# Output bias of the cross attention added on GpSimd, and a new order of the pipelined step, in a one-core decoder layer

## What is computed

```
x = layernorm(x + self_attention(x))            # 16 heads of 8, scores times a decay, softmax
x = layernorm(x + cross(x, ctx))                # below
x = layernorm(x + mixture_of_experts(x))        # layernorm, router, top 2 of 8 experts
cross(q, v):  vp = v @ Wv.T + bv
              A  = softmax(q_h^T k_h / sqrt(128))        # per head, 8 x 8
              out = (vp_h A) @ Wo.T + bo
```

## Time and profile before

| | |
|---|---|
| median of 3 runs | 750.74 us (748.93 to 753.12) |
| the profiled execution | 747.79 us, of which the span in the trace is 746.1 us |
| first block | up to 400 us of the span |
| busy in the span: PE, DVE, ACT, POOL | 573.0, 523.6, 395.0, 393.3 us |
| granted TensorE clock, mean | 0.913 of full speed |

### The profile page before, as it was taken

One profiled execution on the slowest core, in us unless ns is written; L12 is line 12 of the kernel. 1 busy time (PEld: TensorE's weight loads), 2 busy tenths in 40 slices (PEclk: granted clock), 3 DMA queues, 4 the chain that ended last, 5 costly groups with the idle time before them and its releaser, 6 DMA issues. The chain is left out here.

```text
span 746.1 us, 18061 instructions
## 1 busy us (share of the span) xinstructions
PE 573.0 (77%) x5145; PEld 453.1 (61%) x5145; DVE 523.6 (70%) x1567; ACT 395.0 (53%) x1076; POOL 393.3 (53%) x751
## 2 busy tenths in 40 slices
PE   1599999999999999999630698888888888880000
PEld 1256777777777777777520587777777787770000
DVE  1268888888888888888323377677777677760877
ACT  1177888888888888888310344444444444440000
POOL 4073568777777777778670034334344444342444
PEclk9999999999999999999755799999999999995555
DMA  4252121212121211110000555555555555531442
GB/s 149 67 67 66 37 69 48 77 44 73 53 76 48 68 55 45 51 48 17 16 29 7 145 161 170 156 162 163 156 166 165 169 168 160 162 98 34 118 117 84
DMA packets 75650, 70.20 MB, mean 94 GB/s; under 512 B 7809, under 2 KB 58561, under 8 KB 75553
## 3 DMA queue, kind: packets, MB, share of 16 engines
q1 hardware_dynamic: 65264, 55.40, 25.4%
q0 software_dynamic: 5392, 11.01, 5.0%
q10 hardware_dynamic: 4896, 2.64, 1.2%
HBM read 53.85 MB, written 15.17 MB: 93 GB/s over the span
## 5 line engine op out<-in xcount | busy, mean ns | idle before, releaser
L1092 ACT ACTIVATE x2c<-ps_m,prt 128x256 f32<-128x256 f32 x117 | 55.5, 475 | 139.8 <-PE ps_m L1057 139.8
L737 DVE TENSOR_TENSOR sc<-ps_s,decay 128x512 f32<-128x512 f32 x128 | 84.7, 685 | 28.7 <-PE ps_s L522 28.4
L1068 PEld LDWEIGHTS ps_t<-wot,hid 128*128 128x128 f32 x624 | 93.3, 192 | 12.7 <-DVE hid L1128 4.0
L1043 POOL DMA_INDIRECT expert_out<-yt,dest x78 | 82.5, 1057 | 34.0 <-issue 27.8
L1055 PE MATMUL ps_m<-xg,w2t 128*128 128x256 f32 x234 | 73.9, 398 | 32.2 <-DVE hid L1124 29.3
L1068 PE MATMUL ps_t<-wot,hid 128*128 128x128 f32 x624 | 95.8, 277 | 2.7 <-DVE hid L1128 1.9
L522 PE MATMUL ps_s<-kbd,qT 32*128 32x512 f32 x256 | 75.9, 670 | 9.3 <-DMA kbd<-key_image 6.7
L586 ACT ACTIVATE pT<-ps_t 128x512 f32<-128x512 f32 x128 | 72.7, 593 | 16.7 <-PE ps_t L533 16.7
L748 DVE TENSOR_REDUCE rowmax<-sc 128x8 f32<-128x1024 f32 x64 | 78.1, 1220 | 0.4
L659 ACT ACTIVATE sc<-sc,rowmax 128x128 f32<-128x128 f32 x256 | 77.9, 390 | 0.0
L533 PE MATMUL ps_t<-ident,sc 128*128 128x128 f32 x512 | 77.1, 284 | 0.0
(11 more groups left out here) (202 smaller groups left out, 1307.2 us busy)
## 6 DMA issues: line engine op xcount, KB each, us to landing
w2t<-in_L_ffn_W_dram SPq DMA_DIRECT2D x39, 256.0 KB, 2.7
w1t<-in_L_ffn_W_dram SPq DMA_DIRECT2D x39, 256.0 KB, 2.9
wot<-in_L_ffn_Wo_dram SPq DMA_DIRECT2D x39, 256.0 KB, 3.6
kbd<-key_image SPq DMA_DIRECT2D x32, 256.0 KB
xst<-expert_in SPq DMA_DIRECT2D x39, 130.0 KB, 2.1
g<-expert_out SPq DMA_DIRECT2D x32, 128.0 KB, 2.2
call<-in_ctx_dram SPq DMA_DIRECT2D x8, 256.0 KB, 6.5
key_image<-kT SPq DMA_DIRECT2D x32, 64.0 KB, 2.0
```

The costliest lines, as they stand in the source:

```text
L737: dve.tensor_tensor(sc[:, 2 * (b % 2) + i // 2, j:j + 4, :], ps_s[:, i % 2, :, :], decay[:, :].unsqueeze(1).to_broadcast([P, 4, S]), ALU.m ...
L1043: pool.indirect_dma_start(ys_dram[:, :], bass.IndirectOffsetOnAxis(ap=dest[:, n, a:a + 1], axis=0), yt[:, par, a, :], None).then_inc(y_out ...
L1068: mm = pe.matmul(ps_y[par][:, a * P:(a + 1) * P], hid[:, par, c, a * P:(a + 1) * P], wot[:, par, c, :], start=(c == 0 and a == 0), stop=(c ...
```

## The change

The bias is added by POOL: `biased_rows(b)` writes `x1b = x1 + bo_row` into a buffer of its own, with two slots, and `second_sum` has two products in place of three: `oT` with Wo, and `ident` with `x1b`. The matrix `first` and its two memsets go. ACT's `norm1` waits for `x1b_ready` in place of `x_out` before it writes `x1` again.

The lists of all four engines have a new order. On PE the four `mix` and `mix_sums` now stand together behind `score(s + 1, 0)`, and `second_out`, `values`, `ranks`, `second_sum` and `trans_p(s, 0)` follow them; `keys` and `queries` stand later in the step, `trans_p(s - 1, 3)` ahead of `trans_p(s - 1, 2)`. On ACT `norm4` moves from the front to behind `copy_o`, and `copy_p(b, 1)` comes before `copy_p(b, 0)`. On POOL `shift` stands near the end of the list and `router_rows` behind it. The lists of ACT and DVE count their steps from another start; one step more is in the range for that.

```diff
@@ -80,7 +80,6 @@
         router_w = sb("router_w", [P, E])
         ident = sb("ident", [P, P])
         ones = sb("ones", [P, P])
-        first = sb("first", [P, P])
         earlier = sb("earlier", [P, P])
         decay = sb("decay", [P, P])
         wq = sb("wq", [P, D])
@@ -114,6 +113,7 @@
         attT = sb("attT", [P, D])
         st1 = sb("st1", [P, 6]); mv1 = sb("mv1", [P, 2]); rs1 = sb("rs1", [P, 1])
         x1 = sb("x1", [P, 2, D])
+        x1b = sb("x1b", [P, 2, D])
         cT = sb("cT", [P, S])
         vpT = sb("vpT", [P, S])
         gm = sb("gm", [P, D])
@@ -170,7 +170,7 @@
         gram = sem("gram"); gm_ready = sem("gm_ready"); gmax_ready = sem("gmax_ready"); gexp = sem("gexp")
         ginv = sem("ginv"); gA_ready = sem("gA_ready")
         o_done = sem("o_done"); oT_ready = sem("oT_ready"); x_out = sem("x_out")
-        stat2 = sem("stat2"); mean2 = sem("mean2"); eps2 = sem("eps2"); nm_ready = sem("nm_ready"); nm1_ready = sem("nm1_ready"); gained = sem("gained"); scaled = sem("scaled"); rstd2 = sem("rstd2"); x2_ready = sem("x2_ready")
+        stat2 = sem("stat2"); mean2 = sem("mean2"); eps2 = sem("eps2"); nm_ready = sem("nm_ready"); x1b_ready = sem("x1b_ready"); nm1_ready = sem("nm1_ready"); gained = sem("gained"); scaled = sem("scaled"); rstd2 = sem("rstd2"); x2_ready = sem("x2_ready")
         xc_ready = sem("xc_ready"); xf_ready = sem("xf_ready")
         stat4 = sem("stat4"); mean4 = sem("mean4"); eps4 = sem("eps4"); rstd4 = sem("rstd4"); xhat_ready = sem("xhat_ready")
         f_trans = sem("f_trans"); fT_ready = sem("fT_ready"); routed = sem("routed")
@@ -191,7 +191,7 @@
             before(eng, s, min(b, B - 1) + 1)
 
 
-        first_step, last_step = -2, B + 6
+        first_step, last_step = -2, B + 7
 
         with nc.Block() as block:
 
@@ -259,10 +259,7 @@
 
                 pool.memset(shift2[:, 0:1], EPS).then_inc(cst, 1)
                 pool.memset(shift2[:, 1:2], EPS * EPS / (1.0 + EPS)).then_inc(cst, 1)
-                pool.memset(first[:, :], 0.0).then_inc(cst, 1)
-                pool.wait_ge(cst, 11)
-                pool.memset(first[0:1, :], 1.0).then_inc(cst, 1)
-                pool.wait_ge(cst, 12)
+                pool.wait_ge(cst, 10)
 
                 pool.memset(ones[:, :], 1.0).then_inc(rcst, 1)
                 pool.memset(fill[:, :, :], 0.0).then_inc(rcst, 1)
@@ -332,6 +329,11 @@
                     pool.wait_ge(scaled, b + 1)
                     pool.tensor_tensor(xf[:, b % 2, :], xc[:, b % 2, :], offset_row[:, :], ALU.add).then_inc(xf_ready, 1)
 
+                def biased_rows(b):
+                    pool.wait_ge(x1_ready, b + 1)
+                    before(pool, x_out, b - 1)
+                    pool.tensor_tensor(x1b[:, b % 2, :], x1[:, b % 2, :], bo_row[:, :], ALU.add).then_inc(x1b_ready, 1)
+
                 def choices(b):
                     pool.wait_ge(oh_ready, b + 1)
                     before(pool, ranked, b)
@@ -362,16 +364,17 @@
                                                 xhat[:, b, :], None).then_inc(scattered, 16)
 
                 for s in range(first_step, last_step + 1):
-                    if ever(s - 7): place(s - 7)
-                    if ever(s - 6): tag(s - 6)
-                    if ever(s): shift(s)
                     if ever(s - 3): rstd2_of(s - 3)
+                    if ever(s - 5): rstd4_of(s - 5)
                     if ever(s - 7): scatter(s - 7)
                     if ever(s - 6): count(s - 6)
+                    if ever(s - 6): place(s - 6)
+                    if ever(s - 5): choices(s - 5)
+                    if ever(s - 1): rstd1_of(s - 1)
+                    if ever(s - 2): biased_rows(s - 2)
+                    if ever(s - 5): tag(s - 5)
+                    if ever(s + 1): shift(s + 1)
                     if ever(s - 3): router_rows(s - 3)
-                    if ever(s - 5): choices(s - 5)
-                    if ever(s - 4): rstd4_of(s - 4)
-                    if ever(s - 1): rstd1_of(s - 1)
                     if s == 0:
                         with nc.allow_non_contiguous_dma(reason="parameters of one element per partition, once"):
                             pool.dma_start(params[:, :, 0:1], eg.rearrange("e (p a) -> p e a", a=1)).then_inc(ld_e, 16)
@@ -502,10 +505,8 @@
                     upto(pe, logits_read, s - 6)
                     pe.wait_ge(oT_ready, b + 1)
                     pe.matmul(m2a, oT[:, :], xwoT[:, :], start=True, stop=False)
-                    if b == 0:
-                        pe.wait_ge(cst, 12)
-                    pe.matmul(m2a, first[:, :], bo_row[:, :], start=False, stop=False)
-                    pe.matmul(m2a, ident[:, :], x1[:, b % 2, :], start=False, stop=True).then_inc(x_out, 1)
+                    pe.wait_ge(x1b_ready, b + 1)
+                    pe.matmul(m2a, ident[:, :], x1b[:, b % 2, :], start=False, stop=True).then_inc(x_out, 1)
 
                 def score(b, pair):
 
@@ -555,29 +556,29 @@
                     mm.then_inc(mixed, 1)
 
                 for s in range(first_step, last_step + 1):
-                    if ever(s - 6): trans_f(s)
+                    if ever(s - 1): trans_p(s - 1, 1)
                     if ever(s + 2): trans_x(s)
                     if ever(s - 3): trans_c(s)
+                    if ever(s - 6): trans_f(s)
                     if ever(s): score(s, 1)
-                    if ever(s - 1): trans_p(s - 1, 1)
+                    if ever(s - 1): trans_p(s - 1, 3)
+                    if ever(s - 3): gram_of(s)
+                    if ever(s - 3): vp(s)
+                    if ever(s - 6): logits(s)
+                    if ever(s - 1): trans_p(s - 1, 2)
                     if ever(s + 2): keys(s)
-                    if ever(s - 3): gram_of(s)
-                    if ever(s - 6): logits(s)
-                    if ever(s - 3): vp(s)
+                    if ever(s - 2): project(s)
                     if ever(s + 2): queries(s)
-                    if ever(s - 1): trans_p(s - 1, 2)
-                    if ever(s - 1): trans_p(s - 1, 3)
-                    if ever(s - 2): project(s)
+                    if ever(s + 1): score(s + 1, 0)
                     if ever(s - 1): mix(s - 1, 0)
                     if ever(s - 1): mix(s - 1, 1)
+                    if ever(s - 1): mix(s - 1, 2)
+                    if ever(s - 1): mix(s - 1, 3)
+                    if ever(s - 1): mix_sums(s - 1)
+                    if ever(s - 3): second_out(s)
                     if ever(s): values(s)
-                    if ever(s - 3): second_out(s)
-                    if ever(s + 1): score(s + 1, 0)
-                    if ever(s - 1): mix(s - 1, 2)
                     if ever(s - 6): ranks(s)
                     if ever(s - 3): second_sum(s)
-                    if ever(s - 1): mix(s - 1, 3)
-                    if ever(s - 1): mix_sums(s - 1)
                     if ever(s): trans_p(s, 0)
 
             @block.scalar
@@ -672,7 +673,7 @@
                 def norm1(b):
                     act.wait_ge(projected, b + 1)
                     act.wait_ge(nm1_ready, b + 1)
-                    before(act, x_out, b - 1)
+                    before(act, x1b_ready, b - 1)
                     before(act, gram, b - 1)
                     act.activation(x1[:, b % 2, :], m0a, ACT.Identity, bias=nm1[:, 0:1], scale=rs1[:, 0:1]).then_inc(x1_ready, 1)
 
@@ -693,24 +694,24 @@
                     act.activation(gex[:, :], gm[:, :], ACT.Exp, bias=gmax[:, 0:1], accum_out=gsum[:, 0:1]).then_inc(gexp, 1)
 
                 for s in range(first_step, last_step + 1):
-                    if ever(s - 4): copy_vp(s - 4)
-                    if ever(s - 7): norm4(s - 7)
-                    if ever(s - 4): gram_exp(s - 4)
-                    if ever(s + 1): copy_k(s + 1)
-                    if ever(s + 1): copy_q(s + 1)
-                    if ever(s - 4): second_weights(s - 4)
-                    if ever(s - 2): copy_p(s - 2, 2)
-                    if ever(s - 2): copy_p(s - 2, 3)
-                    if ever(s - 4): copy_o(s - 4)
-                    if ever(s - 1): exp_heads(s - 1)
-                    if ever(s - 3): norm1(s - 3)
-                    if ever(s - 1): copy_v(s - 1)
-                    if ever(s - 1): exp_half(s - 1)
-                    if ever(s - 6): copy_f(s - 6)
-                    if ever(s + 2): copy_x(s + 2)
-                    if ever(s - 3): copy_c(s - 3)
-                    if ever(s - 1): copy_p(s - 1, 0)
-                    if ever(s - 1): copy_p(s - 1, 1)
+                    if ever(s - 3): copy_p(s - 3, 0)
+                    if ever(s - 3): copy_p(s - 3, 3)
+                    if ever(s - 5): copy_vp(s - 5)
+                    if ever(s - 3): copy_p(s - 3, 2)
+                    if ever(s - 5): gram_exp(s - 5)
+                    if ever(s): copy_k(s)
+                    if ever(s): copy_q(s)
+                    if ever(s - 5): second_weights(s - 5)
+                    if ever(s - 2): exp_heads(s - 2)
```

(63 more changed lines are left out.)

## The result

The changed kernel takes 755.67 us (median of 7, 754.25 to 761.41), the kernel before 749.60 (7 runs, 748.53 to 753.12): a ratio of 1.009, interval 1.007 to 1.012. The forecast was 734.7. The profiled execution of after, at 761.41 us with a span of 759.1, was the slowest of the seven, so I read its pattern and not its total. The chip that the result was measured on is not on record.

The account below looks back on a forecast made before the run. PE's list was taken to bound the step, falling from 10.17 to 9.52 us; 24 steps gain 15.6, steps 3 to 5 and 30 0.6 each, steps 31 and 32 lose 0.8: 16.0 saved, 734.7 us, range 728 to 744.

Parts of the forecast that it names:

- DVE has 8.88 of work and no more of it: VectorE's work in a step of 10.17 us was counted as 8.88 us, with nothing added by the change.
- Bias product: On PE in `second_sum`: removing the bias product and its two loads was to save 0.22 us a step.
- Regrouped mixing: On PE: mixing products in one group, with fewer switches of array mode, go from 2.58 to 1.83, saving 0.75 us a step.
- the wait for `oT`: On PE ahead of `second_sum`: ACT's `copy_o` is no longer covered, adding 0.27 to PE's list of 9.25, step 9.52.
- The first steps: Parameters' 11 DMAs on POOL now follow `shift(1)`, not `shift(0)`: taken as nothing, from -1.5 to +3 us.
- The keys' way: Keys' store and load between steps: 9.0 us available instead of 11.5, some 8.2 needed, so costed at nothing.
- the case that I had kept for the range: Keys' store and load at 3.46 + 6.15 = 9.6 us, which misses the 9.0 us available by 0.6.
- rival 4: Keys come late in every step before `score(s + 1, 0)`: step 10.7, 13 us lost, 764 us; chance 0.06.
- POOL's 9.01 of work: POOL's list goes from 8.55 to 9.01 us a step with the 0.46 add, still under the step of 9.52.
- The chance of 0.07 for slower: Chance given to a measured time over 754.5 us, against 0.83 for faster and 0.10 for same.

## Why the prediction was wrong

**The step that failed: "DVE has 8.88 of work and no more of it".** I counted DVE's instructions at their old durations. The new lists put `shift1` inside POOL's `shift`, where in most steps it takes 1.41 to 1.8 and not 0.14. DVE is busy for 9.49 a step in after (227.64 / 24), and for 8.92 with `shift1` moved on chip 2 (214.18 / 24). On one chip its place is worth 7.1 us (758.63 against 751.52). The Trainium skill says it (GPSIMD Engine Reference, Key points, on the page I had cited for another rule): GpSimd "Shares its SBUF interfaces with VectorE", with contention for VectorE instructions with two SBUF inputs. The Trainium skill (SBUF — State Buffer, Terms) makes it a lock that is held for the whole instruction. The traces agree: `shift1` ends within 0.03 us of GpSimd's instruction, and takes 0.20 in the form with one tensor input.

**The second thing was in no step, since no view of before named it as a cost.** The forecast took it for granted that a reader starts as soon as PE's product is done. `project`, `keys` and `queries` were moved to stand beside POOL's second scatter issue. On chips 12, 14 and 15 their signals come up to 1.2 us late there. Same kernel, chip 12 against chip 2: 1.001 against 0.985 of before, or 0.3 us won in place of 11.1. This is the larger of the two, and its mechanism stays open. In the trace of before one reader is as late (0.57 behind L478's end at 170.95, beside an issue that ends at 170.85), and single ones of that size stand in traces of chip 2 too. None is on the keys' way.

**How the sum comes out.** Forecast: -16. With shift1 moved, on chip 2: -11.1. The same kernel on chip 12: -0.3, so that the late signals take 10.8. With shift1 back in its place there: +6.8, so that the hold takes 7.1. In the result: +6.1. These are differences of measured times; they share the loss out and don't check the account. What the hold costs the changed kernel where no signal is late was not run. Of the 4.9 us between -16 and -11.1, the trace shows most: it is 3.6 later than that of before when the 24 steps begin, and they win 13.1 and not 15.6.

The forecast's own terms, read where neither effect is present:
- Bias product, 0.22: measured 0.23. Right.
- Regrouped mixing and the wait for `oT`, step 9.52: 9.57 in most steps, 9.62 as the mean. From slot to slot the wait is 0.31 (101.38 less 100.85 + 0.22) where 0.27 was forecast, and the rest is 9.26 where 9.25 was. Right in size, 0.1 small in the mean; 24 x 0.1 = 2.4 us of the sum. That this wait alone holds the step is not so: without it the step is 9.67.
- The first steps, "I take nothing", bound +3: the first `second_sum` comes at 69.5 to 70.0 in the best traces with the new order (73.0 in that of after) where it came at 66.12. Mis-sized: +3.4 against that trace, though the other traces with the old order have it at 65.7 to 68.0. With the parameters' DMAs a step earlier it comes at 70.5, so that they are the cause is not shown.
- The keys' way, cost nothing: right on chip 2. On the others the case that I had kept for the range comes up, 3.46 + 6.15 = 9.6, which "doesn't fit": 3.63 + 5.83 is the row above. It is rival 4's mechanism, in some steps only, set off by the late copy.
- POOL's 9.01 of work: in no trace the bound. That a VectorE add is better (the rule of the Trainium skill, GPSIMD Engine Reference, Engine selection, that I weighed) was not tried and was not what decided; what GpSimd's instructions do to the others beside them was. The sum itself came in time: on chip 2 with `shift1` moved, no wait of PE stands at the product that reads `x1b`. Whether the add delays `shift` behind it, and with it a ring, is not shown.

The chance of 0.07 for slower was too low because my rivals were all waits that the program's semaphores set. Neither cause is such a wait: one is booked as busy time, the other begins behind a product that is over.

## What to carry to other kernels

Before a reordering is priced from old durations, list for each VectorE instruction with two SBUF tensors what GpSimd does at its new time; a tiny one inside a 1.9 us GpSimd instruction costs the rest of that. A maximum far over the median in a line's durations, such as 139/142/1101, is the warning. Give such an instruction its second factor as a scalar operand, or place it elsewhere. And measure an order on more than one chip: the one with `shift1` moved is 1.5% faster on chip 2 and no faster on chips 12 and 15.

## What the runs showed of the hardware

- A VectorE instruction of one element per partition with two SBUF tensors that starts inside a GpSimd instruction ends with it, also when GpSimd has one input (861 ns inside a copy of 1.03 us). The form with one tensor and a per-partition scalar takes 0.20 there.
- By the records PE's completion signals come 0.4 to 1.2 us late beside the end of a GpSimd indirect DMA issue, on chips 12, 14 and 15 and in the trace of after, and not on 2 and 13 but for single ones (0.57). That the issue, or the transfer that it starts, brings it about is shown by taking it out (step 9.98 to 9.63) and by moving it. Why in some groups and not in others, whether it is the chip itself, and by what path, is open; no run here tells.
